# Four residual layers with per-batch weights in fp32r splits: per-tile converting of layer 2, an earlier first split, and LoRA rows in batch, rank, group order

## The reference

```python
x = x + x @ W0.T + b0 + scale0[i0] * (x @ A0[i0].T) @ B0[i0].T     # 8 adapters, rank 16
x = x + x @ W1.T + b1 + (x @ A1[i1].T) @ B1[i1].T                  # 32 adapters, rank 16
x = x + x @ W2[i2].T                                               # 8 full matrices, 1024 x 1024
x = x + einsum('bct,bcd->bdt', x, W3[i3])                          # 16 matrices, 64 x 64, over the rows
```

## Time and profile before

| | |
|---|---|
| median of three runs | 655.12 us |
| profiled execution, its own time | 655.87 us |
| its span, first to last instruction | 653.7 us |
| PE busy | 612.1 us, 94% |
| DVE, ACT, POOL busy | 46%, 33%, 8% |
| mean granted TensorE clock | 0.967 of full |
| DMA | 73.61 MB, 113 GB/s over the span |

### The profile page before, as it was taken

How to read it: one execution, slowest core, us unless ns; L and a number is a source line. 1 busy time by engine, 2 the same in 40 slices (tenths; PEclk the granted TensorE clock), 3 DMA queues, 4 the chain that set the end, 5 groups by cost and what they waited for, 6 DMA issues and landing times.

```text
span 653.7 us, 10849 instructions
## 1 busy us (share of the span) xinstructions
PE 612.1 (94%) x2834; PEld 505.4 (77%) x2835; DVE 297.5 (46%) x554; ACT 214.4 (33%) x306; POOL 50.3 (8%) x87
## 2 busy tenths in 40 slices
PE   5999999999938999999999998999998989999994
PEld 4888878888827888878888887888887756888882
DVE  4992211040464558254356724544863473534210
ACT  3642211040351346222335422323642352333021
POOL 4220001000010011000002100000200030000000
PEclk7999999999987999999999998999999798999997
DMA  7655723021057325733323473233348342221102
GB/s 267 228 181 59 87 82 131 31 84 65 1 181 160 120 63 192 203 100 107 97 85 109 162 227 100 77 102 101 125 134 214 107 160 81 66 87 29 34 2 66
DMA packets 70620, 73.61 MB, mean 113 GB/s; under 512 B 43586, under 2 KB 51778, under 8 KB 70596
## 3 DMA queue, kind: packets, MB, share of 16 engines
q1 hardware_dynamic: 70596, 73.32, 38.8%
HBM read 62.03 MB, written 11.27 MB: 112 GB/s over the span
## 4 chain that ended last, share of the span: by engine, by line
issue 46%; PE 37%; DMA 6%; DVE 3%; POOLq 3%; SPq 2%; POOL 1%; ACT 1%; DVEq 0%; ACTq 0%
PE y_ps L975 10%; PE y_ps L1023 6%; PE t_ps L975 5%; PE y_ps L1052 4%; PE y_ps L957 3%; DMA arena<-wt 3%; POOLq L215 2%; DMA arena<-d_tab 2%; PE t_ps L957 2%; DVE ring L820 2%; PE low_ps L957 2%; PE t_ps L1074 1%; PE low_ps L1014 1%; PE t_ps L966 1%; POOL arena L428 1%
## 5 line engine op out<-in xcount | busy, mean ns | idle before, releaser
L1052 PE MATMUL y_ps<-ring,ops 128*128 128x512 f32 (+1 forms) x792 | 188.3, 394 | 4.0 <-DVE ring L820 3.9
L1023 PE MATMUL y_ps<-wm,ops 128*128 128x512 f32 x768 | 183.7, 396 | 0.0
L1052 PEld LDWEIGHTS y_ps<-ring,ops 128*128 128x128 f32 (+1 forms) x792 | 145.5, 186 | 38.5 <-DVE ring L820 4.8
L1023 PEld LDWEIGHTS y_ps<-wm,ops 128*128 128x128 f32 x768 | 146.1, 192 | 30.5
L975 PE MATMUL y_ps<-ring,wm 128*128 128x512 f32 x240 | 55.3, 390 | 0.0
L820 DVE TENSOR_TENSOR ring<-arena,ring 128x1024 fp32r<-128x1024 f32 x40 | 48.1, 1250 | 14.0 <-ACT ring L526 12.5
L778 DVE SCALAR_TENSOR_TENSOR ops<-arena,b_is_lo,ops 128x1040 fp32r<-128x1040 f32 x16 | 20.8, 1299 | 73.9 <-ACT ops L520 73.9
L975 PEld LDWEIGHTS y_ps<-ring,wm 128*128 128x128 f32 x240 | 44.9, 188 | 9.3
L526 ACT CAST ring<-arena 128x1024 fp32r<-128x1024 f32 x40 | 40.5, 1049 | 24.8 <-POOL arena L428 23.7
L766 DVE TENSOR_TENSOR ops<-arena,ops 128x512 fp32r<-128x512 f32 x32 | 21.9, 691 | 55.3 <-ACT ops L504 55.3
L520 ACT ACTIVATE ops<-arena,b_sign 128x1040 fp32r<-128x1040 f32 x16 | 18.7, 1166 | 82.6 <-DMA arena<-d_tab 81.3
(11 more groups left out here) (143 smaller groups left out, 572.5 us busy)
## 6 DMA issues: line engine op xcount, KB each, us to landing
arena<-wt SPq DMA_DIRECT2D x48, 512.0 KB, 5.4
arena<-b_tab SPq DMA_DIRECT2D x32, 256.2 KB
arena<-xt SPq DMA_DIRECT2D x32, 256.0 KB, 2.9
arena<-b_tab SPq DMA_DIRECT2D x32, 256.0 KB
out<-arena SPq DMA_DIRECT2D x30, 256.0 KB, 3.7
arena<-w SPq DMA_DIRECT2D x8, 576.0 KB, 4.1
a_stage<-a_tab SPq DMA_DIRECT2D x64, 64.0 KB, 1.9
arena<-a_cols SPq DMA_DIRECT2D x8, 256.0 KB, 2.7
```

The lines of the kernel that those rows point to most:

```text
L1023: op = nc.tensor.matmul(y_ps[:, cols], xs[:, k, part_x, :], wm[:, k, part_w, cols], start=k == 0 and part_x == part_w, stop=False)
L1052: op = nc.tensor.matmul(y[0:m, cols], xs2[:, k, part_x, 0:m], ring[:, k, part_w, cols], start=k == 0 and part_x == part_w, stop=k == KT - ...
```

## The change

Four groups of edits:

1. **First split.** A tile's A part has semaphores of its own (`a1_in`, `a1_hi`), so ACT converts it before the W0 tile has landed. W0's high and low part each have a semaphore, and B's too (`b0_hi`, `b0_lo`). PE does the 8 high-by-high matmuls of a tile on `w0_hi`, and the other 16 on `w0_lo`. `start_the_order` moves behind the eight `split_slot`. There are 11 warm-up products in place of 9.
2. **Converting order.** The first matrix is converted two tiles at a time, spread over steps 0 and 1. In mixed steps ACT waits tile by tile (`tile_used`). `quarters` gives way to `tile_used`, `half_used` and `l2_done`.
3. **Layer-3 weights.** `load_w3` stands ahead of `store` in each step and in the tail.
4. **LoRA rows.** The order of partitions and columns is batch, rank, group.

```diff
-WARM_UPS = 9
+WARM_UPS = 11
-MASK_STEPS = 11
+MASK_STEPS = 10
@@ load_b; the other three DMAs of a batch alike
-                    sp.dma_start(b0_stage[r, 0:1 + FEATS], b0_tab[first].unsqueeze(0).to_broadcast(
-                        [GROUPS, RANK, 1 + FEATS])).then_inc(b_in, 16)
+                    sp.dma_start(b0_stage[r, 0:1 + FEATS], b0_tab[first].unsqueeze(1).to_broadcast(
+                        [RANK, GROUPS, 1 + FEATS])).then_inc(b_in, 16)
@@ SP, step and tail
-                    store(j - 2)
                     sp.wait_ge(w3_lo_ready, j - 1)
                     load_w3(j - 1)
+                    store(j - 2)
@@ ACT, first split
             for k in range(KT):
+                act.wait_ge(a1_in[k % STAGES], 16 * (k // STAGES + 1))
+                nc.scalar.copy(a1[:, k, 0, :], slot(k)[:, FEATS + N0_COLS:]).then_inc(a1_hi, 1)
                 act.wait_ge(w0_folded, k + 1)
-                nc.scalar.copy(a1[:, k, 0, :], slot(k)[:, FEATS + N0_COLS:])
-                nc.scalar.copy(w0_blocks(k, 0), ...)
-                nc.scalar.copy(b0_side[:, 0, k, :], ...).then_inc(w0_hi, 1)
+                nc.scalar.copy(w0_blocks(k, 0), ...).then_inc(w0_hi, 1)
+                nc.scalar.copy(b0_side[:, 0, k, :], ...).then_inc(b0_hi, 1)
@@ ACT, a_hi (a_lo on DVE alike)
-                        op = nc.scalar.copy(a_split_of(layer, b)[:, :, 0:GROUPS - 1, :],
-                                            a_of(layer, b).unsqueeze(2).to_broadcast([P, KT, GROUPS - 1, RANK]))
+                        op = nc.scalar.copy(a_split_of(layer, b)[:, :, :, 0:GROUPS - 1],
+                                            a_of(layer, b).unsqueeze(3).to_broadcast([P, KT, RANK, GROUPS - 1]))
@@ ACT
+            def convert_mixed(rank, j):
+                for k in range(KT):
+                    act.wait_ge(tile_used, KT * j + (k + 1))
+                    convert(rank + 1, (k,))
@@ ACT, step (before: all of matrix 0 behind b_hi_parts(1) in step 0)
+                if before == 0:
+                    act.wait_ge(product_done, DONE_M + KT)
+                    convert(0, (0, 1))
                 if not last:
                     a_hi(j + 1)
...
                 if before == 1:
+                    convert(0, (6, 7))
                     xs2_hi(0, 0)
                     xs2_hi(0, 1)
                 if not last:
-                    for h in range(2):
-                        x_hi(j + 1, h)
+                    x_hi(j + 1, 0)
+                    if before == 0:
+                        convert(0, (2, 3))
+                    x_hi(j + 1, 1)
                     b_hi_parts(j + 1)
                 if before == 0:
-                    act.wait_ge(product_done, DONE_M + KT)
-                    convert(0, range(KT))
+                    convert(0, (4, 5))
                     return
...
                 with act.If(mixed != 0):
-                    act.wait_ge(quarters, 4 * j - 3)
-                    convert(rank + 1, FIRST_HALF)
-                    act.wait_ge(quarters, 4 * j - 2)
-                    convert(rank + 1, SECOND_HALF)
+                    convert_mixed(rank, j - 1)
@@ DVE, step
                 low(j, 0)
+                if before == 0:
+                    convert(0, (0, 1))
+                if before == 1:
+                    convert(0, (4, 5))
...
                 low(j, 1)
                 if not last:
                     a_lo(j + 1)
                 if before == 1:
+                    convert(0, (6, 7))
                     xs2_lo(0, 0)
                     xs2_lo(0, 1)
...
-                    convert(0, range(KT))     (step 0; tiles 2 and 3 now stand between the two x_lo)
@@ DVE, g_split: two operations of 64 columns, one per batch, in place of one of 128
@@ PE
             def a1_products():
                 for k in range(KT):
+                    pe.wait_ge(w0_hi, k + 1)
+                    for i in range(KT):
+                        nc.tensor.matmul(PASS1[i], wm[:, i, 0, k * P:(k + 1) * P], a1[:, k, 0, :], start=k == 0, stop=False)
                     pe.wait_ge(w0_lo, k + 1)
                     for i in range(KT):
-                        for part_w, part_a in SPLIT:
+                        for part_w, part_a in SPLIT[1:]:
```

More of the change, by code:

```diff
@@ L183, in build @@
         ones_ready = sem("ones_ready")
+        a1_in = [sem(f"a1_in{n}") for n in range(STAGES)]
         w0_folded, w0_hi, w0_lo = sem("w0_folded"), sem("w0_hi"), sem("w0_lo")
+        a1_hi, b0_hi, b0_lo = sem("a1_hi"), sem("b0_hi"), sem("b0_lo")
         w1_folded, w1_hi, w1_lo = sem("w1_folded"), sem("w1_hi"), sem("w1_lo")
@@ L383, in _ @@
                 first_chunks(rank + mixed + 2)
-            store(PAIRS - 2)
             sp.wait_ge(w3_lo_ready, PAIRS - 1)
             load_w3(PAIRS - 1)
+            store(PAIRS - 2)
             rank, mixed = first_rank(sp, PAIRS - 1), mixed_of(sp, PAIRS - 1)
@@ L456, in a_split_of @@
         def a_split_of(layer, b):
-            return a_split[:, layer].rearrange("p k (b e r) -> p k b e r", e=GROUPS, b=2)[:, :, b]
+            return a_split[:, layer].rearrange("p k (b r e) -> p k b r e", e=GROUPS, b=2)[:, :, b]
         def w0_blocks(k, part):
@@ L772, in a_lo @@
                         split = a_split_of(layer, b)
-                        op = nc.vector.tensor_tensor(split[:, :, A_LO, :], a_of(layer, b), split[:, :, 0, :], ALU.subtract)
+                        op = nc.vector.tensor_tensor(split[:, :, :, A_LO], a_of(layer, b), split[:, :, :, 0], ALU.subtract)
                 op.then_inc(a_lo_ready, 1)
@@ L787, in b_lo_parts @@
                     dve.wait_ge(low_done, 2 * j)
-                nc.vector.tensor_tensor(g_split[:, :].rearrange("p (e r) -> p e r", r=RANK),
-                                        g_mask[:, :].rearrange("p (e r) -> p e r", r=RANK),
-                                        b0_split[:, FEATS:].unsqueeze(1).to_broadcast([KL, 2 * GROUPS, RANK]),
-                                        ALU.mult).then_inc(g_ready, 1)
+                for b in range(2):
+                    cols = slice(b * GROUPS * RANK, (b + 1) * GROUPS * RANK)
+                    op = nc.vector.tensor_tensor(g_split[:, cols].rearrange("p (r e) -> p r e", e=GROUPS),
+                                                 g_mask[:, cols].rearrange("p (r e) -> p r e", e=GROUPS),
+                                                 b0_split[:, FEATS:].unsqueeze(2).to_broadcast([KL, RANK, GROUPS]),
+                                                 ALU.mult)
+                op.then_inc(g_ready, 1)
             def low(j, layer):
@@ L861, in step @@
                 if not last:
-                    for h in range(2):
-                        x_lo(j + 1, h)
+                    x_lo(j + 1, 0)
+                    if before == 0:
+                        convert(0, (2, 3))
+                    x_lo(j + 1, 1)
                 take_x2(j)
@@ L877, in _ @@
             masks()
-            start_the_order()
             for k in range(KT):
                 split_slot(k)
+            start_the_order()
             for k in range(KT):
@@ L963, in g_products @@
                 pe.wait_ge(evictions, 1)
+                pe.wait_ge(b0_lo, KT)
                 for k in range(KT):
@@ L1046, in transposes, with layer2_half @@
                 op.then_inc(t_done, 1)
-            def layer2_half(y, h, m=P, marks=()):
+            def layer2_half(y, h, m=P, tiles=False, final=False):
                 for k in (FIRST_HALF, SECOND_HALF)[h]:
@@ L1053, in layer2_half @@
                                                   start=k == 0 and part_x == part_w, stop=k == KT - 1 and part_x == 1)
-                    if k in marks:
-                        op.then_inc(quarters, 1)
+                            if final and k == HK and part_x == part_w and cols is BANKS[0]:
+                                op.then_inc(half_used, 1)
+                            if tiles and final and k == KT - 1 and part_x == 1 and cols is BANKS[0]:
+                                op.then_inc(tile_used, 1)
+                    if final and k == KT - 1:
+                        op.then_inc(l2_done, 1)
+                    elif tiles:
+                        op.then_inc(tile_used, 1)
             def layer2_by_banks(y, m=P):
@@ L1088, in first_part @@
                     pe.wait_ge(w_lo, rank * KT + HK)
-                    layer2_half(y, 0, marks=marks)
+                    layer2_half(y, 0, tiles=True)
                     between()
@@ L1092, in first_part, with last_part @@
                     pe.wait_ge(w_lo, rank * KT + KT)
-                def last_part(m=P):
+                def last_part(m=P, tiles=False):
                     if last:
@@ L1107, in layer2 @@
                 with pe.Else():
-                    first_part((HK - 3, HK - 2, HK - 1))
-                    last_part()
+                    first_part()
+                    last_part(tiles=True)
             def step(j, before=1):
```

78 lines of the change are left out of this document (38 added, 40 removed).

## The result

| | before | after |
|---|---|---|
| median, the two kernels run side by side | 655.23 us (4 runs) | 617.66 us (4 runs, 617.59 to 618.9) |
| ratio, 95% interval | | 0.9427 [0.9368, 0.9486] |
| profiled execution, its span | 653.7 us | 615.5 us |
| PE busy | 612.1 us | 600.7 us |
| mean granted clock | 0.967 | 0.996 |

The account below looks back on a forecast made before the run. PE, busy 94% of the span, was taken as the bound, with only its waits and the 1.2 GHz stretches behind them removable. Gains of 7.2 + 14.5 + 19 + 5.5 = 46.2 us gave 609.0 us, range 605 to 617.

Parts of the forecast that it names:

- Place 1: First split in the opening: PE starts on high parts alone and keeps the full clock, gaining 7.2 us.
- the second rival: The opening or step 1 finds a new wait: 3 to 7 us given back, 612 to 616; chance 0.15.
- Place 2: Steps 0 and 1: converting the first matrix earlier removes the 12.17 us wait, gaining 14.5 us, up to 2 less.
- Place 3: Loop, steps 2 to 15: faster LoRA rows and earlier mixed-step tiles win 19 of 20.2 us lost.
- the mixed step: In the loop: ACT starts some 4.5 us sooner, 1 us is left lost, and the step takes 38 us.
- the first rival: LoRA rows don't get faster; the loop gains only about 5 us, total 623; chance 0.06.
- the 0.9 that I had named as a sign: At each `load_b`, a DMA share near 0.9 for a few us would show the forecast right.
- Two more signs: No PE wait above 1 us in steps 0 and 1; ACT's L520 released by PE, not a DMA.
- the lower bound of 14: Smallest gain forecast for the loop, 14 us, if the mixed step's tile waits stay.
- Place 4: Tail: layer-3 weights loaded ahead of `store` gain 5.5 us, bounds 4.5 and 6.
- Costed at nothing: Per step, split `g_split` and strided LoRA copies stay hidden beside PE; uncovered, up to 3 us in each of 14 steps.
- Slower rival: Four neighbouring partitions reading one DRAM row make LoRA rows land later, every step touched: 677 us; chance 0.03.

Follow-up runs that it names:

- the best version: Changed kernel with mixed-step work moved forward on POOL, SP, ACT and DVE, and PE's `xs2_lo` wait put behind its plan reads: 607.85 us, ratio 0.9272.
- run 11: Changed kernel with nine warm-up products in place of eleven: 618.2 us, ratio 0.941.
- Run 5: Changed kernel with PE's wait for `xs2_lo` in step 1 moved behind the reads of the plan: 615.64 us, ratio 0.9372.
- run 1: Kernel before, with only the LoRA rows' order changed to batch, rank, group: 645.51 us, ratio 0.9824.
- run 2: Changed kernel with the LoRA rows put back in batch, group, rank order: 638.71 us, ratio 0.9725.
- Run 7: Changed kernel with ACT waiting by halves in mixed steps, as in the kernel before: 620.42 us, ratio 0.945.
- runs 3, 4 and 9: Changed kernel with POOL folding mixed tiles first, 619.44 us; plus SP loading tiles 4 to 7 earlier, 616.21; plus ACT/DVE converting tiles 0 to 3 earlier, 610.24.
- run 6: Changed kernel with the layer-3 weights loaded behind `store` again, in each step and in the tail: 631.07 us, ratio 0.9597.
- run 12: Changed kernel with the first split's high-by-high products waiting for the low part too: 622.86 us, ratio 0.9481.

## Why the prediction was right or wrong

**The bound** was read rightly: only gaps of PE and the lower clock behind them could be won. In the best version no wait of PE is over 0.72 us behind the warm-ups, and its time is 607.85 us, where the prediction's bounds at their best gave 607.

**Place 1, the opening, right:** 6.7 of 7.2 us. The first products began 0.35 later than worked out. That the two extra warm-ups "fill the gap exactly" was wrong by 0.62 us and of no account: nine did as well (run 11). The full clock through the first tiles came as taken, and no fold held PE up behind its first product. Of the 3 to 7 us that the second rival put on these two places, 1.9 came (0.5 here, 1.4 in place 2).

**Place 2, the first matrix, right in mechanism, off by 1.4 us:** 13.1 of 14.5. (The subtraction started from 207.9, where rows 5 have 208.09; from that row it is 14.8, and 1.7 us are missing.) The prediction named `xs2_lo` as the tightest place and the second rival priced a wait there. The data were in time, by 0.25 us; the gap came all the same, from PE's instructions between the wait and the first matmul, 1.81 us that the prediction did not count. Run 5 took them out.

**Place 3, the LoRA rows, right; the mixed step, wrong.** That the order of the source makes the rows slow is shown by run 1 from one side and run 2 from the other, and the first rival falls with it. The Trainium skill's rule ("DMA: Bandwidth & Descriptors", "Why a DMA increments its semaphore by 16 and not by 1") asked for 16 engines after the change; the share of 0.75 in the window above is more than 4 of 16 can give, so it agrees as far as that; it does not count them. It is also less than the 0.9 that I had named as a sign. Two more signs did not come: no wait above 1 us in steps 0 and 1 (1.81 us, place 2), and ACT's L520 (now L523) released by PE. L523 is still released by a DMA in 7 steps, after up to 3.1 us, because SP issues the last row only then (269.31, with ACT free 3.06 us before 272.36). It costs the unmixed steps nothing. The unmixed steps gave back 6.9 us, all they had lost.

The step that failed is this sentence: "With the waits per tile, and the LoRA rows and layer-3 weights (POOL folds these first) early, ACT can start some 4.5 us sooner". ACT started 10.28 us after layer 2 began (495.72 - 485.44), where before it was 6.88 (526.06 - 519.18). The sentence credits the 4.5 us to the LoRA rows, the layer-3 load and the waits per tile, and nothing in the sum stood for SP's own time before that load. But SP began this turn 4.06 us behind PE and needs 15.46 us from there to the layer-3 load, with no wait in it, however early the rows land. In the kernel before, PE itself was late in this step: from its start at 496.83 it took 22.35 us to layer 2 (519.18), where it takes 15.23 now (470.21 to 485.44). So SP's layer-3 load, issued at 520.40, looked timely, 1.2 us behind PE's layer 2. With PE on time the same load is 4.3 us behind. Of the mixed step, the part up to layer 2 gave back 7.1 us (22.35 - 15.23), and the part from there on became 1.4 longer (28.72 before, 30.12 after), where 5.0 less were forecast. The forecast for the loop was 19 us and 12.6 came, below the lower bound of 14 ("the tile waits stay"), since the waits did not stay but grew; the 6.4 that are missing are all in this step. Run 7 shows that the waits per tile decide nothing as long as the folds are late; runs 3, 4 and 9 show three orders in series, POOL's, SP's, and that of ACT and DVE, of which each hid the next. None of the three rivals names this.

**Place 4, the tail, right:** 5.9 of 5.5. But its edit also works in the mixed step, 5.8 us by run 6, which the prediction had as "costs `store` 1.2 us" and nothing more. Without it the shortfall in the mixed step would have been about twice as large (6.4 + 5.8).

**Costed at nothing:** `g_split` in two operations and the copies with columns four apart stayed hidden: the twelve unmixed steps take 27.00 to 27.05 us. The copies take 512 ns where they took 510.

**Slower rival:** four neighbouring partitions reading one row cost nothing; the rows land some 2 to 3 us after the last issue (269.85 to 272.36), not 10.

**The sum of misses:** 0.5 + 1.4 + 6.4 - 0.4 = 7.9 of span, with 0.7 for the median, which this time does not lie below the profiled execution (617.66 and 617.64).

## What to carry to other kernels

Once a bottleneck engine loses its own delay, whatever was issued at a fixed pace looks late: measure each feeding queue's own turn without its waits (here 24.4 us, and 27.3 with four tiles to load, against PE's 27.0), and how far behind it begins, before calling its work early. In a chain of engines that each have a fixed program order, follow the late tile through all of them and move it forward in every one; moving it in one only shifts the wait. And put a wait behind the register reads that the waiting engine needs, not ahead of them.

## What the runs showed of the hardware that was not expected

- **Reading a plan costs a sequencer time.** A register load from the table took 264 to 988 ns on SP, median 268, and there are 16 in a turn. Behind a wait such reads are bare: 1.81 us on PE at 188.22, 2.33 us on POOL at 495.23.
- **The clock and short gaps.** PE idled 1.33 us before its first product in run 11, and 1.81 us before 188.22 in the kernel after, and the clock stayed at 1.00; 2.29 us in run 12 were followed by 0.50. Behind one and the same wait of 4.1 us in the mixed step the loss in slow matmuls was not the same: 2.0 us in the kernel after and 1.8 in run 11 (45.01 - 37.9 - 5.30), but 3.2 in run 5 (45.24 - 37.9 - 4.18) and 3.4 in run 12 (46.25 - 37.9 - 4.99). It does not go by whether a second, shorter wait follows: run 12 has one (0.90 us), run 5 has none. What decides it stays open.
- **A fold of POOL beside busy DVE** can take many times its 0.46 us. Two rows of the timeline of the kernel after, and POOL's fold line from 30 to 42 us (count: shortest/median/longest ns):

```profile
33.28 5.68 POOL L424 TENSOR_TENSOR arena<-arena,ident 128x128 f32<-128x128 f32 x2 [2.55 <-DMA arena<-wt]
...
36.95 1.26 DVE L760 SCALAR_TENSOR_TENSOR arena<-arena,b_sb 128x1024 f32<-128x1024 f32 x1
```
```profile
L424 POOL TENSOR_TENSOR arena<-arena,ident x5: 453/469/5259, 30.3 to 41.6; 128x128 f32<-128x128 f32 x5
```

  So one of the two took 5.26 us and the other its usual time, while DVE's instructions there take 1.2 to 1.3 us each. The long one ends at 38.54, 0.33 us after the last instruction of an unbroken run of DVE (38.21). In the kernel before it is the same: one of the two folds at 11.37 took 3.68 us and ended at 15.05, 0.33 us after DVE's run ended (14.72). So in both the fold lasted for as long as DVE had one instruction behind the other. The Trainium skill ("SBUF — State Buffer", "SBUF: two separate sides") has the pair of ports locked for one instruction at a time; these rows show more than the wait for one. It cost PE nothing here, since W1's tiles are wanted later; ACT waited 6.75 us for the fold.
